# Turning the experts' middle rows one block deeper: one TensorE step and its partners on ScalarE and VectorE move to another place in the block loop

## The reference, cut to what matters

```python
E, K, I = (64, 8, 192)
logits = x @ gate_weight.T
scores = softmax(logits, axis=-1)
topk_w, topk_idx = jax.lax.top_k(scores, K)
topk_w = topk_w / sum(topk_w)
order = jnp.argsort(topk_idx.reshape(-1))
sorted_tokens = jnp.repeat(x, K, axis=0)[order]
g = ragged_dot(sorted_tokens, w_gate, group_sizes)
u = ragged_dot(sorted_tokens, w_up, group_sizes)
out = ragged_dot(silu(g) * u, w_down, group_sizes)
y = sum(out[inv].reshape(-1, K, h) * topk_w[:, :, None], axis=1)
```

## Time and profile before

| what | us |
|---|---|
| median of the runs | 1591.69 |
| the profiled execution | 1591.39 |
| its span | 1589.6 |
| TensorE busy | 1417.3 (89%) |
| VectorE busy | 1032.6 (65%) |
| ScalarE busy | 903.5 (57%) |
| POOL busy | 610.6 (38%) |

### The profile page before, as it was taken

One profiled execution on the slowest core, in us unless ns is written; L12 is line 12 of the kernel. 1 busy time (PEld: TensorE's weight loads), 2 busy tenths in 40 slices (PEclk: granted clock), 3 DMA queues, 4 the chain that ended last, 5 costly groups with the idle time before them and its releaser, 6 DMA issues. The chain is left out here.

```text
span 1589.6 us, 37709 instructions
## 1 busy us (share of the span) xinstructions
PE 1417.3 (89%) x8673; PEld 1192.5 (75%) x8674; DVE 1032.6 (65%) x2067; ACT 903.5 (57%) x2048; POOL 610.6 (38%) x704
## 2 busy tenths in 40 slices
PE   7999899989734999999999999999943599999999
PEld 5887566657523898888888898888841488888888
DVE  5555588866686676676776766666635476667632
ACT  5555699864294666666666666666621244444442
POOL 1222487751241322322332232222226566666322
PEclk9999799999855999999999999999976799999999
DMA  6221790001261587878787877877537444444200
GB/s 218 80 87 54 286 356 29 2 5 60 85 273 60 194 287 264 285 242 292 258 276 245 292 236 251 273 261 241 191 131 259 139 145 139 136 122 126 77 14 28
DMA packets 93281, 278.16 MB, mean 175 GB/s; under 512 B 12757, under 2 KB 12886, under 8 KB 92502
## 3 DMA queue, kind: packets, MB, share of 16 engines
q1 hardware_dynamic: 69526, 199.67, 35.6%
q0 software_dynamic: 23680, 77.61, 16.1%
HBM read 209.07 MB, written 76.81 MB: 180 GB/s over the span
## 5 line engine op out<-in xcount | busy, mean ns | idle before, releaser
L1185 POOL DMA_INDIRECT xg<-h_rows,idx x168 | 182.7, 1087 | 465.1 <-PE m_x L1213 457.2
L1228 PE MATMUL m_g<-wgu_high,bxTh 128*128 x660 | 235.9, 357 | 2.0 <-DVE bxTl L1301 1.8
L1228 PE MATMUL m_g<-wgu_low,bxTh 128*128 x660 | 223.3, 338 | 0.0
L1228 PE MATMUL m_g<-wgu_high,bxTl 128*128 x660 | 223.0, 338 | 0.0
L1631 PE MATMUL f_g<-x4T_high,ffn_gu 128*128 128x256 f32 x704 | 175.4, 291 | 13.9 <-DVE f_hid L1803 12.2
L1631 PE MATMUL f_g<-x4T_low,ffn_gu 128*128 128x256 f32 x704 | 168.9, 281 | 0.0
L1301 DVE TENSOR_TENSOR bxTl<-m_x,bxTh 128x512 fp32r<-128x512 f32 x166 | 114.7, 691 | 83.3 <-ACT bxTh L1370 72.5
L1063 DVE TENSOR_TENSOR wgu_low<-raw_gu,wgu_high x61 | 107.3, 1758 | 81.4 <-ACT wgu_high L1053 66.5
L1388 ACT ACTIVATE y<-m_y 128x512 f32<-128x512 f32 x164 | 98.2, 599 | 106.6 <-PE m_y L1248 87.6
L1522 POOL DMA_INDIRECT G<-y_rows,slot x128 | 132.5, 1035 | 55.8 <-issue 50.5
L1248 PE MATMUL m_y<-wd_high,hidTm 128*128 x328 | 143.9, 439 | 7.5 <-issue 3.9
(11 more groups left out here) (264 smaller groups left out, 3267.0 us busy)
## 6 DMA issues: line engine op xcount, KB each, us to landing
raw_gu<-in_exp_gu SPq DMA_DIRECT2D x64, 768.0 KB, 6.8
y_rows<-y SPq DMA_DIRECT2D x164, 256.0 KB
raw_d<-in_exp_d SPq DMA_DIRECT2D x64, 512.0 KB, 7.6
y_rows<-zero SPq DMA_DIRECT2D x64, 256.0 KB, 3.5
ffn_gu<-ffn_gu_words SPq DMA_DIRECT2D x1, 5632.0 KB, 22.4
raw_c<-in_ctxT SPq DMA_DIRECT2D x16, 256.0 KB, 2.7
X<-in_x SPq DMA_DIRECT2D x4, 1024.0 KB, 6.1
h_rows<-h SPq DMA_DIRECT2D x16, 256.0 KB, 2.0
```

What stands on the lines that cost most here:

```text
L1185: eng.indirect_dma_start(xg[:, u, :].bitcast(F32), None, h_dram, bass.IndirectOffsetOnAxis(ap=idx[half][:, u:u + 1], axis=0)).then_inc(s_g ...
L1228: m = eng.matmul(pg[u % 2][:, 0:2 * I], xT[l][:, u % 2, c, :], W.gu[r][:, buf * DC + c, :], start=c == 0 and n == 0, stop=c == DC - 1 and ...
```

## The change

`turn_hidden` of a block moves one step of the loop later on TensorE, and in that step it stands directly behind `turn`, ahead of `gate_up`. `lows` on VectorE and `highs` on ScalarE move from near the end of their step to the start of the next one. A last `turn_hidden`, `highs` and `lows` follow after the loops. VectorE's first group, once the first pass of a hardware loop, is now written out ahead of it; the OR into `low_bits` stays at the end of a group.

```diff
@@ TensorE
                 turn(b + 2, (u + 2) % GB, i + 1 + (u + 2) // GB)
+                if before is not None:
+                    turn_hidden(b - 1, (u - 1) % GB)
                 gate_up(b + 1, (u + 1) % GB, *following, needed)
 
                 after = entry(eng, b + 2)
-                turn_hidden(b, u)
                 if before is not None:
                     down(b - 1, (u - 1) % GB, *before)
...
-            down(eng.snap(used * GB - 1, min_val=T * K // P - 1, max_val=NBLK - 1), GB - 1, *taken()[0])
+            last = eng.snap(used * GB - 1, min_val=T * K // P - 1, max_val=NBLK - 1)
+            turn_hidden(last, GB - 1)
+            down(last, GB - 1, *taken()[0])
@@ VectorE
-            def one(b, u, before):
+            def one(b, u, before, first):
+                if not (first and u == 0):
+                    lows(b - 1, (u - 1) % GB)
                 turned(b + 2, u + 2)
                 e = begun(eng, b - 1)
                 split_next(eng, before, b - 2, W.low_d)
                 split_next(eng, e, b - 1, W.low_gu)
                 hidden(b + 1, u + 1)
-                lows(b, u)
                 return e
 
-            def group(i):
+            def bits_of(i, chunk):
+                dveB.wait(eng, i - 1, "bits")
+                dveB.done(eng.tensor_tensor(low_bits[:, :], low_bits[:, :], all_bits[:, bass.ts(chunk, D)], ALU.bitwise_or), "bits")
+
+            def blocks(i, first):
                 before = begun(eng, i * GB - 2)
                 for u in range(GB):
-                    before = one(i * GB + u, u, before)
+                    before = one(i * GB + u, u, before, first)
+
+            def group(i):
+                blocks(i, False)
                 with eng.If(i < 2 * FC):
...
+                    bits_of(i, eng.snap(i % (2 * FC), min_val=0, max_val=2 * FC - 1))
...
+            blocks(0, True)
+            bits_of(0, 0)
+            begin = WORDS_AT[0]
...
+            lows(eng.snap(used * GB - 1, min_val=T * K // P - 1, max_val=NBLK - 1), GB - 1)
@@ ScalarE
             def one(i, u, before, first):
                 b = i * GB + u
+                if not (first and u == 0):
+                    highs(b - 1, (u - 1) % GB)
                 turned(b + 2, u + 2)
...
                 silu(b + 1, u + 1)
-                highs(b, u)
                 if not (first and u == 0):
                     out(b - 1, (u - 1) % GB, None if first and u < 3 else i * 32 + (u + 1) // 2 * 16)
...
+            highs(last, GB - 1)
             out(last, GB - 1, eng.snap(used * 32, min_val=T * K // P * 8, max_val=NBLK * 8))
```

More of the change, by code:

```diff
@@ L1334, in one @@
                 hidden(b + 1, u + 1)
-                lows(b, u)
                 return e
-            def group(i):
+            def bits_of(i, chunk):
+                dveB.wait(eng, i - 1, "bits")
+                dveB.done(eng.tensor_tensor(low_bits[:, :], low_bits[:, :], all_bits[:, bass.ts(chunk, D)], ALU.bitwise_or), "bits")
+            def blocks(i, first):
                 before = begun(eng, i * GB - 2)
                 for u in range(GB):
-                    before = one(i * GB + u, u, before)
+                    before = one(i * GB + u, u, before, first)
+            def group(i):
+                blocks(i, False)
                 with eng.If(i < 2 * FC):
-                    dveB.wait(eng, i - 1, "bits")
-                    dveB.done(eng.tensor_tensor(low_bits[:, :], low_bits[:, :], all_bits[:, bass.ts(eng.snap(i % (2 * FC), min_val=0, max_val=2 * FC - 1), D)], ALU.bitwise_or), "bits")
+                    bits_of(i, eng.snap(i % (2 * FC), min_val=0, max_val=2 * FC - 1))
             used = used_groups(eng, endb)
-            begin = 0
+            blocks(0, True)
+            bits_of(0, 0)
+            begin = WORDS_AT[0]
             for r, chunks in enumerate(rounds):
-                with eng.Fori(begin, WORDS_AT[r]) as i:
-                    group(i)
+                if begin < WORDS_AT[r]:
+                    with eng.Fori(begin, WORDS_AT[r]) as i:
+                        group(i)
                 eng.wait_ge(s_words[r], 16 * len(chunks))
```

## The result

| what | before | after |
|---|---|---|
| median of the runs, us | 1591.16 (4 runs, 1589.09 to 1591.76) | 1618.34 (4 runs, 1616.48 to 1620.44) |
| ratio, 95% interval | | 1.0158 (1.0130 to 1.0186) |
| span of the profiled execution | 1589.6 | 1615.7 |
| 162 steps of the block loop, from the first `m_g` of one step to that of the next | 647.1 | 670.3 |
| start of the last `m_g` product to the end of the last `m_y` | 9.61 | 13.17 |

The kernel became 1.6% slower: 1612 was forecast with a range of 1596 to 1630, and 1618.3 was measured, inside it. Of the 26.1 us by which the span grew, 23.2 lie in the steps of the loop and 3.6 behind the last `m_g`.

The account below looks back on a forecast made before the run. TensorE was taken as the bound, and in disturbed blocks the chain `wgu_high`, `wgu_low`, `hid`, `hidTm` to the down product. Terms 5.3 + 0.8 + 1.0 + 1.3 + 8.3 + 3.2 + 1.4 = 21.3 us on 1591.39 gave 1612.7, stated 1612, range 1596 to 1630.

Parts of the forecast that it names:

- Nothing is won where the wait at `m_h` goes: TensorE: the 12.5 us wait at `m_h` goes, but `m_y` still waits for the same lows; term 0.
- ScalarE's order: ScalarE: `hidTm` now behind `y`, ahead of `bxTh` and the splits, delays disturbed blocks by 0.26 us each; 5.3, 1.0 and 1.3 us.
- TensorE's sequencer at a group's end: Five groups' last blocks where lows end late: the sequencer reaches the next `m_x` late, 0.26 us each; 1.3 us.
- the sequencer starves: Rival: TensorE's sequencer, held longer at the down product, is late at groups' ends or every block; 1620 to 1646, chance 0.10.
- Group's first block: ScalarE, held by loop registers, starts `hidTm` at 1.48, making `m_y` 0.05 us late in 17 groups; 0.8 us.
- ORs behind the remainders: VectorE between groups: lows now stand behind `low_bits` and the operation on `spares`, delaying `m_y` in nine groups; 8.3 us.
- The store of y: ScalarE: `hidTm` now stands behind `y`, which waits for an earlier store; four of 15 waits delay `m_y`; 3.2 us.
- Packing: TensorE: fewer entries from short to long matmuls per block; bounds 0 and -13 us, taken as 0.
- packing wins: Rival: TensorE's matmuls pack closer by 13 us while waits still grow by 21, giving 1599; chance 0.15.
- Tail: At the last down product, turn, ScalarE's copy and VectorE's lows run one after another with nothing beside them; 1.4 us.

Follow-up runs that it names:

- the first experiment: The changed kernel with VectorE's ORs into `low_bits` and on `spares` behind the remainders of a group's second step: 1622.87 us, ratio 1.0140 to the kernel before.
- the second: The changed kernel with the table read at a group's start moved behind the first step's work on ScalarE and VectorE: 1629.49 us, ratio 1.0181.
- the last kernels: Changed kernel with `wgu_low` one step later, alone and with two additions (1.0297, 1.0318, 1.0369); kernel before with `wgu_low` last, `y` behind `bxTh` (0.9968).
- The last kernel: The kernel before with `wgu_low` last in VectorE's step and ScalarE's `y` behind the next step's `bxTh`: 1589.60 us against 1595.67, ratio 0.9968.

## Why the prediction was right in sum and off in its parts

The terms add up to 21.3 us; the span grew by 26.1. That this landed inside the range is in part luck: the wait for late operands at `m_y` came close (18.6 forecast in five of the terms, about 20 measured, though not term by term), while a term for the sequencer was far too small and one for packing had been put at nothing, and these two errors have opposite signs.

- *Nothing is won where the wait at `m_h` goes.* Right: 12.5 us of it vanished, and the wait moved to `m_y`.
- *ScalarE's order, 5.3 + 1.0 + 1.3 = 7.6.* D, E and F together grew by 7.8, but not where I put it. The 20 waits of the earlier trace rows are D, which I priced at +5.3 (20 x 0.26 is 5.2) and which fell by 4.2. The longer first step ahead of it gives ScalarE and VectorE time to catch up: behind the five first steps of over 4.3 us D took 4.0 on average, behind the other fifteen 4.6. E and F, priced at 2.3, cost 12.0. One step that failed is the 0.26 per block: counted from `m_x`, `wgu_high` went from 1.65 to 2.14 (medians), that is 0.49. `hidTm` waits for its turn, which ends behind the four of `m_x`, and so follows `y` by 0.55 to 0.62 and not by 0.48 (0.49 where the middle rows are turned first); `bxTh` follows that by 0.28 (853.49, 854.11, 854.39 above). From `y` to `bxTh` it is 0.83 in the median where it was 0.48, and 0.14 more lies between `bxTh` and the split. The sum of this term is right by two errors against each other.
- *TensorE's sequencer at a group's end, 1.3 of these.* This is the other error. I had priced 0.26 us in five blocks. The 13 steps of F alone lose 6.3 us more than before between `m_y` and the next `m_g`, some 0.5 us each, and all steps together about 10. My rival *the sequencer starves* had this mechanism and a chance of 0.10; it came true at the groups' ends after `wgu_low`, and not in the quiet blocks. In F most of the loss is here and not at `m_y` (2.3 us).
- *Group's first block, 0.8.* Mis-sized by 6 us or more: B and C grew by 7.9, of which the first experiment takes 0.9 to the ORs and the second 5.1 to the registers. I had seen the registers' 0.61 of idle time and set `hidTm` at 1.48; it starts at 1.58, `m_y` at 2.94 and not at 2.66. In the kernel after:

```profile
865.28 0.60 ACT L1402 ACTIVATE y<-m_y 128x512 f32<-128x512 f32 x1 [0.92 <-PE m_y L1248]
866.58 0.39 ACT L1396 ACTIVATE hidTm<-m_h 128x256 fp32r<-128x256 f32 x1 [0.70 <-issue]
```

```profile
865.00 0.46 PE L1213 MATMUL m_x<-identr,xg 128*128 128x128 f32 x4
...
867.94 0.49 PE L1248 MATMUL m_y<-wd_high,hidTm 128*128 x1
```

  The remainders end at 2.69 here; 0.25 more passes until `m_y`, not the 0.15 of a second or third step; why is not shown.
- *ORs behind the remainders, 8.3.* Right in size and place: 9.0 at A in the first experiment, 11 steps where I had counted 9. (The text ahead of the prediction reads as if the 11 groups with an OR on `spares` were among the 22 with one into `low_bits`; two of them are not, so 24 groups have an OR.)
- *The store of y, 3.2.* Not seen: the waits for it fell from 18.9 to 7.2 us. I kept their place from one trace though I had written that it differs from run to run. A longer step gives the stores more time, which would fit, but no run separates this from what else SP's queue and the transfers do. In the kernel before with `wgu_low` last they grew to 41.3. (The `y` at 869.44 starts 2.4 us after its `m_x` at 867.07, not 2.1; the term took 0.35 for it and does not change.) The Trainium skill ("TensorE: Matmul & The Clock Gate", section "Architectural detail: the array is 16× 32×32, not 1× 128×128") states the strict order of ScalarE's queue, and the trace agrees: `bxTh` starts at 613.43 behind `y` at 612.22, while its `m_x` had begun at 609.00. The rule holds, but it doesn't say how often a store is late.
- *Packing, 0 of 0 to -13.* Mis-sized: the entry from short to long matmuls is shorter by 0.08 at `m_y` (0.48 to 0.40), and 0.03 comes back between the second `m_h` and `m_g`. A step of 3.86 became 3.81: 3.3 us less in G alone, about 8 in all steps, so the rival *packing wins* was right in its mechanism and in 8 of its 13 us. My argument that the long first `m_y` hid the pair's own time was wrong.
- *Tail, 1.4.* It was 3.6: 0.77 until the last turn starts, 2.25 for turn, copies and remainders, and 0.54 because the last `m_y` run slower. In the windows shown above the granted clock fell from 0.71 to 0.50, that is to 1.2 GHz, while TensorE had stood for 4.92 us (in the kernel before it was 1.00 from 1172 to 1174, after 3.94 us of standing, and 0.62 from 1174 to 1177); I had priced the chain at full clock and by its parts' length. The Trainium skill ("Advanced Engine Details and Errata", section "Clock Domains") says that TensorE's array is gated to 1.2 GHz when idle; the trace agrees.

Of the signs that I had named, three came as written: no wait of `m_h` for `hid`, the longest waits where `low_bits` runs behind `wgu_low`, and `hidTm` directly behind `y`. Quiet blocks of 3.81 lie just outside the 3.82 to 3.88 named, towards packing. The weight load of `m_y` waits 81 times, not some 40.

What the experiments show as the common cause is lost lead, that is the time between the end of an operand and the start of its user. In the kernel before, the remainders of a quiet step without any split end 2.5 us ahead of the down product that wants them (0.15 before `m_g`, wanted 2.32 after it), with `wd_low` ahead of them 1.4 us (0.93 for 2.32). In the changed one they end at 1.39 for 2.18 in either case, 0.8 us, and at a group's first step with nothing to spare. The turn of the middle rows gained lead over `hid`, took it from the chain `m_h`, `hidTm`, remainders, `m_y`, and with it the lead that TensorE's sequencer had at a group's end. Moving the copies, the registers or the ORs shifts part of the loss between kinds of steps. None of these orders removes it; the middle rows turned ahead of the gathered ones won back 9.1 of the 23.2 us, the most of all. It was not tried to join the orders that helped, to move `wgu_low` without putting it beside `wd_low`, or to give the change its lead back by a third buffer. Nor is it shown what part of G's growth in the last kernels is SP's later weight transfers.

The version that beats both kernels is the one before with `wgu_low` last in VectorE's step, 0.34% under the kernel before (0.17 to 0.50; with `y` behind `bxTh` as well it is 0.32%, no different), for data without two neighbouring experts of a single block.

## What to carry to other kernels

Moving a step of a software pipeline deeper gives lead to its producers and takes it from its consumers: compare both leads block by block (end of the operand to start of its user) before the move, and move only where the producer's is the short one. Count the sequencer among the consumers: an operand that is just in time can still make what stands behind it at a loop's end late. Where a wait ends on a chain over two other engines, look for the longest instruction on it that nobody wants soon, here a 1.76 us weight split, and put it behind. And price steps by kind (first of a group, after a split, quiet): a sum can come out right while its terms are wrong.

## What the runs showed of the hardware

- Short matmuls between long ones cost by where they stand: an undisturbed step took 3.81 us with four `m_x`, two `m_h`, then `m_g`; 3.82 to 3.87 with the two `m_h` ahead of `m_x`, or between `m_g` and `m_y`.
- Behind a loop's branch and a read of the block table ScalarE stood idle for 0.70 us (put down to the issue) before its next copy. With the branch left there and the read moved, the copy started 0.43 us after `m_g` and not 1.07, so the read is what costs. On VectorE 0.66 us went by before a split that stands behind such a read inside a step.
- At a group's end, where TensorE's operand was done only 0.15 us before the down product, the next `m_x` followed that product's last matmul by 0.62 to 0.71 us (13 times, in the steps of F, put down to the issue). Where the operand was done 0.8 us before, it followed by 0.24, at 27 group ends as well.
- The waits of ScalarE for the store of `y` came to 7.2 us in all at a mean step of 4.14 us, 18.9 at 3.99 and 41.3 at 3.94. The last kernel also has another order on VectorE, so that the step's length is the reason is not shown.
